# A two-layer graph kernel: four of eight x projections moved to the opening loads, and the opening loads reordered

## The reference

```python
A = adj + eye(4096)
d_inv_sqrt = rsqrt(sum(A, axis=1))
A_hat = A * d_inv_sqrt[:, None] * d_inv_sqrt[None, :]
x = layernorm(x + elu((A_hat @ x) @ w))
x = layernorm(x + relu((adj @ x) @ W.T + b))
```

## Time and profile before

| | |
|---|---|
| median of 3 runs | 863.29 us |
| lowest, highest | 862.93, 869.79 us |
| profiled execution, its own time | 869.26 us |
| its span in the trace | 867.3 us |
| PE, DVE, ACT, POOL busy over the span | 792.3, 745.5, 511.8, 190.6 us |
| moved by DMA | 181.71 MB, mean 210 GB/s |

### The profile page before, as it was taken

The page is one execution under the profiler, slowest core; times in us unless marked ns, Lnnn a source line. Parts: engine busy times, 40 slices in busy tenths (PEclk is TensorE's granted clock), DMA queues, the critical chain, the costliest instruction groups (busy, mean ns, idle before and its releaser), DMA issues.

```text
span 867.3 us, 10759 instructions
## 1 busy us (share of the span) xinstructions
PE 792.3 (91%) x3532; PEld 652.6 (75%) x3532; DVE 745.5 (86%) x587; ACT 511.8 (59%) x1132; POOL 190.6 (22%) x181
## 2 busy tenths in 40 slices
PE   0465989799999999999999999999999999999996
PEld 0344768578888888888888888888888888888884
DVE  2368979999889999889998999899898998887962
ACT  1355666566776674578776746576744656446351
POOL 0004353351453600012221001020202223023031
PEclk9977989899999999999999999999999999999998
DMA  9999999789999699799989988898997898997400
GB/s 269 320 320 284 216 172 227 180 205 238 254 269 287 144 216 222 210 201 224 212 215 240 208 217 190 188 226 189 211 271 169 205 225 191 213 220 182 102 24 25
DMA packets 183590, 181.71 MB, mean 210 GB/s; under 512 B 6768, under 2 KB 183536, under 8 KB 183536
## 3 DMA queue, kind: packets, MB, share of 16 engines
q1 hardware_dynamic: 94704, 93.21, 46.0%
q10 hardware_dynamic: 88832, 87.83, 42.9%
HBM read 176.82 MB, written 4.19 MB: 209 GB/s over the span
## 4 chain that ended last, share of the span: by engine, by line
PE 62%; DVE 1%; ACT 0%; issue 0%; POOLq 0%; POOL 0%; ACTq 0%; DVEq 0%
PE acc L992 19%; PE acc L994 19%; PE acc L993 19%; PE proj L948 3%; PE proj L946 1%; PE proj L927 0%; ACT acc L481 0%; DVE turned L644 0%; PE acc L969 0%; DVE stats L854 0%; DVE raw L848 0%; PE acc L1025 0%; ACT a_hi L471 0%; DVE v_lo L699 0%; ACT normed L628 0%
## 5 line engine op out<-in xcount | busy, mean ns | idle before, releaser
L992 PE MATMUL acc<-a_hi,v_hi 128*128 128x512 f32 x1024 | 408.9, 399 | 20.5 <-DVE a_lo L659 11.0
L471 ACT ACTIVATE a_hi<-turned 128x1024 fp32r<-128x1024 f32 x256 | 264.4, 1058 | 264.0 <-PE acc L994 134.8
L993 PE MATMUL acc<-a_lo,v_hi 128*128 128x512 f32 x1024 | 403.7, 394 | 0.0
L994 PE MATMUL acc<-a_hi,v_lo 128*128 128x512 f32 x1024 | 403.6, 394 | 0.0
L659 DVE TENSOR_TENSOR a_lo<-turned,a_hi 128x1024 fp32r<-128x1024 f32 x256 | 321.1, 1291 | 32.5 <-ACT a_hi L471 23.4
L644 DVE STREAM_TRANSPOSE turned<-raw 128x2048 f32<-128x2048 f32 x122 | 280.0, 2302 | 6.1
L992 PEld LDWEIGHTS acc<-a_hi,v_hi 128*128 128x128 f32 x1024 | 195.5, 191 | 64.1 <-issue 13.5
L994 PEld LDWEIGHTS acc<-a_hi,v_lo 128*128 128x128 f32 x1024 | 195.3, 191 | 41.6
L993 PEld LDWEIGHTS acc<-a_lo,v_hi 128*128 128x128 f32 x1024 | 195.6, 191 | 40.2
L481 ACT ACTIVATE acc<-raw 128x256 f32<-128x256 f32 x198 | 73.0, 369 | 20.6 <-DMA raw<-in_adj_dram 11.7
L666 DVE TENSOR_REDUCE deg_parts<-raw 128x4 f32<-128x1024 f32 (+3 forms) x29 | 43.0, 1483 | 21.3 <-DMA raw<-in_adj_dram 21.3
(11 more groups left out here) (69 smaller groups left out, 408.2 us busy)
## 6 DMA issues: line engine op xcount, KB each, us to landing
raw<-in_adj_dram SPq DMA_DIRECT2D x154, 512.0 KB, 9.1
raw<-in_adj_dram ACTq DMA_DIRECT2D x154, 512.0 KB, 9.8
x_row<-in_x_dram SPq DMA_DIRECT2D x64, 128.0 KB, 5.4
out_dram<-normed ACTq DMA_DIRECT2D x28, 128.0 KB, 3.3
held<-in_adj_dram ACTq DMA_DIRECT2D x4, 512.0 KB, 13.0
held<-in_adj_dram SPq DMA_DIRECT2D x4, 512.0 KB, 13.0
partial<-in_adj_dram ACTq DMA_DIRECT2D x2, 512.0 KB, 19.0
partial<-in_adj_dram SPq DMA_DIRECT2D x2, 512.0 KB, 18.4
```

Source lines behind the costliest of these rows:

```text
L471: nc.scalar.activation(a_hi[u % 2][:, part, :], turned[u % 2][:, part, :], ACT.Copy).then_inc(s_hi, 1)
L992: pe.matmul(dst, v_hi[:, k, ch], a_hi[u % 2][:, t, :], start=begin, stop=False)
L993: pe.matmul(dst, v_hi[:, k, ch], a_lo[u % 2][:, t, :], start=False, stop=False)
L994: ins = pe.matmul(dst, v_lo[:, k, ch], a_hi[u % 2][:, t, :], start=False, stop=end)
```

## The change

Five things change.

1. x of groups 4 to 7 is loaded by ACT behind its halves of chunks 2, 3, 4 and 7 (`X_AFTER`), straight into `raw[2]`, which holds four such tiles (`xw`). PE turns and projects them during chunks 2 to 8 (`turn_x_ahead`, `project_x_ahead`) through the PSUM tile `acc[1]` (group 7: `proj`), and ACT copies each twice, the turned x (`keep_xt_ahead`) and the product (`keep_xw_ahead`), back into its place in `xw`. `make_y` and `y_low` of groups 4 to 7 read `xw` instead of `proj`, and the turning, copying and projecting in rows 4 to 7 is gone.
2. `raw[2]` leaves the ring: phase A has three ring buffers and, for chunks 10 to 14, home buffer 5. Only chunk 12 gets it.
3. x of group 0 is loaded half by SP and half by ACT right after chunk 1; w follows it on SP's queue. W and b are loaded after chunk 3.
4. W is turned at chunk 4 instead of ahead of everything, and `keep_wt` moves from chunk 1 to chunk 4.
5. Some waits are restated for the new owners of the buffers.

```diff
-    RING = (0, 1, 6, 2)
+    RING = (0, 1, 6)
+    SPARE, SPARE_FROM, SPARE_TO = 5, 10, 14
...
-            for i in RING if n <= FIRST_B else RING[:3]:
+            for i in RING + ((SPARE,) if SPARE_FROM <= n <= SPARE_TO else ()):
...
+    X_AFTER = {2: 4, 3: 5, 4: 6, 7: 7}
...
+        xw = [raw[2][:, GT * i:GT * (i + 1), :] for i in range(GROUPS - FAST)]
...
+        def ahead_bank(row):
+
+            whole = proj[:] if row == GROUPS - 1 else acc[1][:]
+            return bass.AP(whole.tensor, whole.offset, [list(whole.ap[0]), [1, GT * C]])
...
-                if m >= 1 and m <= GROUPS:
+                if m >= 1 and m < FAST:
                     sp.wait_ge(s_xw, m)
+                elif m == GROUPS:
+                    sp.wait_ge(s_xw, FAST)
...
-                for q in range(STRIPES):
+                for q in range(STRIPES) if m else (0, 1):
                     sp.dma_start(x_row[B32 * q:B32 * (q + 1), :, :], nodes_part(x, m % GROUPS, q)).then_inc(s_x, 16)
...
+                for m in x_loads_after[n]:
+                    load_x(m)
                 if n == 1:
                     sp.dma_start(w_sb[:], w.rearrange("(h c) n -> c h n", h=CH)).then_inc(s_w, 16)
-                    sp.dma_start(normed[:, 0:CH, :], W.rearrange("(h c) n -> c h n", h=CH)).then_inc(s_w, 16)
-                    sp.dma_start(b_sb[:], b.rearrange("(a n) -> a n", a=1).to_broadcast([P, C])).then_inc(s_w, 16)
-                for m in x_loads_after[n]:
-                    load_x(m)
+                if n == PANELS - 1:
+                    sp.dma_start(normed[:, 0:CH, :], W.rearrange("(h c) n -> c h n", h=CH)).then_inc(s_wb, 16)
+                    sp.dma_start(b_sb[:], b.rearrange("(a n) -> a n", a=1).to_broadcast([P, C])).then_inc(s_wb, 16)
...
-                act.wait_ge(s_xw, row + 1)
-                if row >= FAST:
+                if row < FAST:
+                    act.wait_ge(s_xw, row + 1)
+                    whole = proj[:]
+                else:
+                    act.wait_ge(s_xwk, row - FAST + 1)
                     act.wait_ge(s_turn, max(units_through[n] for n in HOMES))
+                    whole = xw[row - FAST]
                 for t in range(GT):
-                    ins = nc.scalar.activation(v_hi[:, tiles(row).start + 2 * t, :], proj[:, t, :], ACT.Copy,
+                    ins = nc.scalar.activation(v_hi[:, tiles(row).start + 2 * t, :], whole[:, t, :], ACT.Copy,
...
+            def keep_xt_ahead(row):
+
+                act.wait_ge(s_xet, row - FAST + 1)
+                nc.scalar.activation(xw[row - FAST].rearrange("p t n -> p (t n)"), ahead_bank(row), ACT.Copy).then_inc(s_xek, 1)
+
+            def keep_xw_ahead(row):
+
+                act.wait_ge(s_xep, row - FAST + 1)
+                nc.scalar.activation(xw[row - FAST].rearrange("p t n -> p (t n)"), ahead_bank(row), ACT.Copy).then_inc(s_xwk, 1)
...
                 elif row >= FAST:
-                    act.wait_ge(s_turn, max(units_through[n] for n in HOMES))
+                    raw_free(act, LAST_SPARE)
...
+                    if m in X_AFTER:
+                        load_x_ahead(X_AFTER[m])
...
+            def load_x_ahead(row):
+
+                for q in range(STRIPES):
+                    act.dma_start(xw[row - FAST][B32 * q:B32 * (q + 1), :, :], nodes_part(x, row, q)).then_inc(s_xe[row - FAST], 16)
+
             for n in range(AHEAD):
                 load_chunk(act, n, (2, 3))
+                if n == 1:
+                    for q in (2, 3):
+                        act.dma_start(x_row[B32 * q:B32 * (q + 1), :, :], nodes_part(x, 0, q)).then_inc(s_x, 16)
+                if n in X_AFTER:
+                    load_x_ahead(X_AFTER[n])
...
+                if n in (6, 7):
+                    keep_xw_ahead(n - 1)
...
+                    if n == 9 and u == visits[n][0]:
+                        keep_xw_ahead(7)
...
+                if n == 3:
+                    keep_xw_ahead(4)
+                if n in (2, 4, 6):
+                    keep_xt_ahead(4 + (n - 2) // 2)
+                if n == 8:
+                    keep_xt_ahead(7)
+                if row < FAST and at == 1:
                     keep_xt(row)
...
+                whole = proj[:] if row < FAST else xw[row - FAST]
+                if row >= FAST:
+                    dve.wait_ge(s_xwk, row - FAST + 1)
...
-                    nc.vector.scalar_tensor_tensor(out=v_lo[:, k, :], in0=proj[:, t, :],
...
-                if n == 1:
+                if n == PANELS:
                     keep_wt()
...
+            def turn_second_weights():
+
+                pe.wait_ge(s_wb, 32)
+                pe.wait_ge(s_y, GT)
...
+            def turn_x_ahead(row):
+
+                pe.wait_ge(s_xe[row - FAST], 64)
+                if row == GROUPS - 1:
+                    pe.wait_ge(s_y, GT * 2)
+                elif row > FAST:
+                    pe.wait_ge(s_xwk, row - FAST)
+                flat = ahead_bank(row)
...
+            def project_x_ahead(row):
+
+                pe.wait_ge(s_w, 16)
+                pe.wait_ge(s_xek, row - FAST + 1)
...
+                if row == 1:
+                    pe.wait_ge(s_wt, 1)
+                if row == 2:
+                    pe.wait_ge(s_xwk, GROUPS - FAST)
...
+                pe.wait_ge(s_w, 16)
...
+                    if bank_of[a] == 1:
+                        pe.wait_ge(s_xwk, GROUPS - FAST - 1)
...
+                if n == PANELS:
+                    turn_second_weights()
+                    turn_x_ahead(5)
                 if row < FAST and at == 1:
                     turn_x(row)
+                if n == 5:
+                    project_x_ahead(5)
                 if row < FAST and at == 2:
                     project_x(row)
+                if n == 2:
+                    turn_x_ahead(4)
+                if n == 6:
+                    turn_x_ahead(6)
+                if n == 7:
+                    project_x_ahead(6)
                 if row < FAST and at == 3:
                     fold_degrees(row)
+                if n == 3:
+                    project_x_ahead(4)
                 for u in visits[n]:
                     if row >= FAST and u == last_in_a[row]:
                         fold_degrees(row)
                     product(u)
-                if row >= FAST and at == 2:
-                    turn_x(row)
-                if row >= FAST and at == 3:
-                    project_x(row)
+                if n == 7:
+                    turn_x_ahead(7)
+                if n == 8:
+                    project_x_ahead(7)
             for u in range(visits[FIRST_B][0], U):
```

45 lines of the change are left out of this document (28 added, 17 removed).

## The result

| | before | after |
|---|---|---|
| median (runs) | 866.17 us (4) | 881.10 us (4) |
| lowest, highest | 862.93, 869.79 us | 879.32, 883.76 us |
| ratio, 95% interval | | 1.0167 [1.0141, 1.0193] |
| profiled execution, its span | 869.26, 867.3 us | 883.76, 881.7 us |

The forecast was 869 us with a range up to 877: slower was right, by how much was not. The table that this document reads most cuts each profiled span at three marks, the starts of DVE's degree sums of groups 1, 3 and 7. The last column is the rest of the span.

The account below looks back on a forecast made before the run. It took DMA to bound the kernel up to 73 us, then from 190 to 326 us PE with DVE close behind. Terms -6 + 10.9 + 1 = +5.9 us, on 863.3 gave 869 us, range 854 to 877.

Parts of the forecast that it names:

- ACT held in its issues: Opening: 14 x pieces issued ahead of chunk 1's degree part on ACT start it 10.6 us later, at 35.4.
- rival A: Opening: ACT's issues do not hold it, so it costs 0 to 4.6 us; 858 to 863 us, chance 0.20.
- Do the bytes arrive?: Opening: by a byte count at 304 GB/s chunk 7 still lands near 67 us, so DMA is not last.
- Rival D: Opening: projections of groups 0 and 1 slip and SP's queue runs dry, adding 2 to 5 us; 871 to 874, chance 0.06.
- the chain between PE and ACT: Opening: alternating turns, copies and projections after group 0's fold put group 1's sum at 82.5 instead of 71.62, +10.9 us.
- Group 7 and group 2: Between units 2 and 3: group 7's turn and projection, 4.7 us, delay group 2's fold by about +1 us (0 to 3).
- rival C: Chunks 11 to 17: three buffers starve DVE, 4 us for each of two chunks; 877 us, chance 0.12.
- The late gain of -6: Rows 4 to 7 and handover to phase B: removed x work gains 2.5 and 3.6 us, -6.1, taken as 6.
- The handover: Start of phase B: PE's lag of 3.6 us, with group 7's projection in between, goes.
- ACT's lateness of 2.5 us goes: Rows 4 to 7: PE's backlog makes ACT late, so DVE's 2.5 us of waits for ACT's degree part vanish.
- the 97% named as a sign: Rows 4 to 7: if the forecast is right, PE has gaps and DVE is busy 97% or more.
- Rival B: Rows 4 to 7: PE is the bound, so all 18.6 us go; 857 us with the forecast's opening, chance 0.12.

Follow-up runs that it names:

- h3: g3 with x of groups 4 to 7 split, partitions 0 to 63 loaded by SP and 64 to 127 by ACT; 866.83 us, 0.9993.
- f1: The changed kernel with its loads, ring and order, but nothing turned, copied or projected ahead (product with w left out for groups 4 to 7); 877.73 us, 1.0140.
- g3: f1 with ACT copying group 0's turned x behind the degree part of chunk 0 instead of chunk 1; 869.63 us, 1.0030.
- h1: g1 with its first two chunks crossed, so both queues write the same half of the partitions at the same time; 869.10 us, 1.0031.
- e2: The changed kernel with group 6's projection and its copy moved behind group 1's fold and chunk 7's degree part; 879.75 us, 1.0154.
- f3: e2 with ACT copying group 0's turned x behind chunk 0's degree part instead of chunk 1's; 876.56 us, 1.0115.
- h2: The changed kernel with early copy of group 0's turned x, group 1's fold before group 6's steps, and x ahead split between both queues; 873.47 us, 1.0078.
- f2: The kernel before with only parts 3 and 4 of the change, the reordered loads of the opening and W's later turn; 863.78 us, 0.9970.
- g1: f2 with ACT copying group 0's turned x behind the degree part of chunk 0; 862.96 us, 0.9952.
- e3: The kernel before with only the changed ring, three buffers and home buffer 5 for chunks 10 to 14; 865.84 us, 0.9999.
- e4: The kernel before with x of groups 4 to 7 neither loaded, turned nor projected; 866.03 us, 0.9990.
- e1: The changed kernel with x of groups 4 to 7 issued by SP instead of ACT, behind SP's halves of the same chunks; 880.59 us, 1.0161.
- h4: g1 with x of group 1 split between SP and ACT as well; 860.54 us, 0.9936.
- g2: f1 with x of groups 4 to 7 loaded behind chunks 8 to 11 instead of 2, 3, 4 and 7; 872.70 us, 1.0068.

## Why the prediction was wrong

The forecast was 863.3 + 5.9 = 869 us, measured were 881.10. Of the 12 us between them 2.9 are the starting value: the kernel before has a median of 866.17 over four runs, 863.29 over the first three. The change itself was forecast at 5.9 us and came to 14.9.

**ACT held in its issues: the term that was too small.** The mechanism and its place at the head of the opening were right. Forecast for the degree part of chunk 1: 35.4 us; measured 39.43, so the 14 pieces cost 14.7 us and not 10.6. The forecast priced them by their bytes at half of 348 GB/s. That rate was not there: 212 to 279 GB/s from 24 to 28 us, 213 from 36 to 39. h3 shows that the price was sound and the rate was wrong. There 8 such pieces stand ahead of the part, split by halves; the forecast's way of counting gives 24.77 us and 1.05 MB at 174 GB/s, 30.8 us (an estimate from these numbers; the early copy is not in it), and that copy takes 1.00 us in front of it; the part starts at 31.77. The late start passes on to the fold of group 0, 54.25 for 50.7. A second hold had no term in the sum at all: group 7's four pieces stand in the middle of the chain and hold ACT for 4.84 us at 60.82, so the copy of group 5's turned x, which PE has ready at 66.6, starts at 68.17 (forecast 63.9). The Trainium skill's sentence ("DMA: Bandwidth & Descriptors", "Issuing engines are not separate DMA queues") that issuing is "usually small relative to the DMA itself" is not borne out here: four pieces of 128 KB held ACT for 7.06, 6.65 and 4.84 us, more than the 3.0 us in which a queue moves their bytes at 174 GB/s, and rival A that rested on it was wrong.

**"Do the bytes arrive?": the step that failed.** The forecast counted bytes against the joint rate and let chunk 7 land where it did, near 67. It landed at 77.30. The count holds only while both queues are fed and write different halves of the partitions, and the change broke both. First, the late copy of group 0's x made its projection late (ended 49.5), SP's queue stood behind that projection and ran out, and what was left wrote one half: f1 has sum 1 at 85.9 without any chain, g3 at 77.2 with one copy moved. Second, ACT's pieces of x for partitions 0 to 63 met SP's chunk halves: h3, which splits them, has 74.1, and h1 shows the effect by itself. Rival D had the first mechanism by name: "SP's queue, which waits for those, runs dry". It was given 0.06 and 2 to 5 us, and it is 8.7 of f1's 14.3. The forecast had the number for it: it moved the copy of group 0 to 37.9 in one sentence and did not ask who else waits for the projection behind it. Of the second it knew nothing.

**Which of the two set the sum of group 1.** In the changed kernel the chain between PE and ACT ended last, as forecast. Its steps came in the order and with the durations forecast (projections 3.69 us, copies 1.02), and it carried the +4 us of ACT's holds through to the sum: 86.8 against 82.5. The landing was the second path, 4.8 us behind: e2 takes the last steps out of the way, and the sum then stands at 82.0 behind chunk 7's landing at 77.02, 10.4 us later than before, where the forecast had nothing. So either path alone made the opening late. Both go back to the 348 GB/s that were taken as given: at a lower rate ACT is held longer and the chunks come later. Early copy alone gains 1.3 us at sum 1 over e2 (f3); with the split the sum falls another 6.3, to 74.4 (h2).

**Group 7 and group 2.** Forecast +1. From sum 1 to sum 2 the kernel before took 37.7 us, f1 (no chain) 37.5, the changed one 41.5 and h2 44.3: +3.8 to +6.6. DVE's waits there are in front of `a_lo` (2.9 us in the changed kernel, 6.9 to 7.7 in e2, f3 and h2, 0.5 in before and f1) and for chunk 11 (2.0 to 2.2 us, 0.5 in f1, none before). The second is the sign named for rival C, once and at a quarter of its 8 us. The changed kernel has paid it back before sum 3, and part of that belongs to the reordered opening: f2 and g1 take 71.8 and 71.9 us from sum 1 to 3 against 75.3 to 78.8 in before, e3 and e4. Why they do is left open.

**The late gain of -6.** The handover gave -4.3 us (forecast -3.6). At the place foreseen 2.3 are found: from sum 7 to the product behind phase A it took 9.4 us and now takes 7.0; where the other 2.0 come from was not looked into, and the other kernels without late x work give -1.1 to -4.3. Rows 4 to 7 should have given -2.5, because "ACT's lateness of 2.5 us goes". It did not go: DVE's degree sums wait 2.2 us for ACT in the changed kernel, 2.5, 3.8, 2.2 and 2.3 in e1, e2, f3 and h2, which run the same code there. PE's backlog was not what made ACT late there. DVE was busy 91% of rows 4 to 7, not the 97% named as a sign.

In this profiled execution the stage is even 5.3 us longer. Of these 1.1 are busy time of DVE (159.9 for 158.8 us) and 4.2 are idle, mainly 4.0 us for PE's fold of group 3 where it was 2.0, and 4.6 in front of `a_lo` where it was 2.0. The 5.3 is not steady: e1, e2, f3 and h2 take 169.4 to 172.3 us, and before, e3, f2, g1, h1 and h4, which all have the late work, 170.5 to 173.1. Read over all of them, the gain is nothing within 3 us either way.

The lengthening of DVE's own work, put down to POOL above, is e4's alone: there the mean `a_lo` is 1394 ns, in the changed kernel 1332 against 1344 before; that a relieved PE causes it was not tested by itself. `y_low` from SBUF, for which the trace had no row, takes 587 ns instead of the 478 from PSUM, 1.3 us for the 12 that are read there; the bound was 1. Rival B, which made PE the bound, is dead by e4: 18.6 us off PE and at most some 2 us gained. Its time is given as 857 us in the list of rivals and as 854 where the range is set; nothing hangs on it.

**The sum.** To sum 1 +15.2 for +10.9; to sum 3 -1.8 for +1; to sum 7 +5.3 for -2.5; after that -4.3 for -3.6: 14.4 for 5.9. By size the error is 4.3 in the opening and 7.8 in rows 4 to 7, less 3.5 in the other two. The opening's error is the one of ACT's holds, the one without a term among them. Of the 7.8 only 1.4 to 4.3 come back in the other kernels with this code, whose rows 4 to 7 lie 3.5 to 6.4 us lower; that is the 2.5 of ACT's lateness, give or take the spread, and the rest was not met again.

## What to carry to other kernels

Counting bytes against the joint rate holds only while every queue is fed and the queues write different halves of the partitions: split a load between two queues as the loads beside it are split, and when a step is delayed, ask which queue waits for it. Small DMAs put into the program of a computing engine cost it the backlog of its queue, not their own size alone. Before moving work off a full engine, leave it out altogether once: e4 would have said that there was next to nothing to win.

## What the runs showed of the hardware

- **Half of the partitions, 0.6 of the rate.** 211 to 220 GB/s in h1, where both queues were set to write one half, against 345 in g1 from 8 to 14 us with one queue in each half. The slow stretches of the changed kernel, with one queue or with two, had 203 to 236, its fast ones 340 to 353. The share of busy DMA was 1.12 to 1.14 in the slow case and 1.10 to 1.11 in the fast one.
- **The same four issues, 1.74 to 7.06 us.** Four pieces of 128 KB took 1.74 us to issue on SP after a pause, and 1.96 (g2, at 86.22) to 7.06 us on ACT with a filled queue.
- **DVE and POOL.** In e4's rows two-operand instructions of both at once take 1.8 and 2.0 times as long (4.16 for 2.32 us, 1.74 for 0.88). Not every overlap lengthens both: POOL's wider row just before, at 226.66, runs beside the same pair and takes 1.55 us, like most such rows of this trace.
- **TensorE's clock.** Behind a wait of 4.67 us at 257.47 in the changed kernel, the passes of 512 columns start 0.43 us apart up to 263.4 us, and 0.23 apart from 264 on. The granted clock of the two stretches is 0.50 and 1.00, the levels of 1.2 and 2.4 GHz. The row of the wait, then the two windows:

```profile
257.47 0.28 PE L986 MATMUL acc<-deg_sums,fold 128*32 128x4 f32 x8 [4.67 <-DVE deg_sums L736]
```

```profile
257.50:263.40 5.90, 5.90 (x21) 4.65 (x22) 5.90 (x4) 2.14 (x3) 0.00 (x0) 0.50 0.85 229
264.00:266.00 2.00, 2.00 (x10) 1.61 (x10) 2.00 (x4) 0.32 (x1) 0.65 (x1) 1.00 0.94 280
```
